# First half of the maximum scores between the transposes and the main scores, fewer VectorE instructions a step, and one pipeline stage less, in a gated cross-attention and expert layer

## What is computed

```python
x = x + tanh(g_xattn[0]) * xattn(values=ctx, keys=ctx, query=layernorm(x), w_out, b_out)
#   energy = einsum('nqhd,nkhd->nhqk', q, k);  softmax(energy / sqrt(128)) over k;  out @ w_out.T + b_out
x = x + tanh(g_ffn[0]) * ffn(layernorm(x), Wg, W1, b1, W2, b2)
#   logits = xt @ Wg; idx1, idx2 = the two best experts of a row, weighted by their gates
#   pos1 = rows before this one whose first choice is the same expert   (a running count)
#   pos2 = the same for second choices, behind all the first ones;  rows past C = 2048 are dropped
#   h = gelu(xe @ W1 + b1); ye = h @ W2 + b2; out = w1 * ye[idx1, pos1] + w2 * ye[idx2, pos2]
```

## Time and profile before

| what | value |
|---|---|
| time, median of 3 runs | 402.06 us (400.1 to 402.23) |
| time of the profiled execution | 403.13 us |
| its span in the trace | 401.3 us |
| busy in the span: TensorE matmul, VectorE, ScalarE, GpSimd | 79%, 68%, 56%, 55% |

### The profile page before, as it was taken

The page is one execution under the profiler, slowest core; times in us unless marked ns, Lnnn a source line. Parts: engine busy times, 40 slices in busy tenths (PEclk is TensorE's granted clock), DMA queues, the critical chain, the costliest instruction groups (busy, mean ns, idle before and its releaser), DMA issues.

```text
span 401.3 us, 13831 instructions
## 1 busy us (share of the span) xinstructions
PE 315.7 (79%) x4010; PEld 255.9 (64%) x4011; DVE 274.2 (68%) x1088; ACT 223.6 (56%) x660; POOL 222.2 (55%) x368
## 2 busy tenths in 40 slices
PE   0488999999999999977405999999999989998200
PEld 0246666666666666655304899999999989997100
DVE  4758999999999999975762455554555545554287
ACT  1358887777777778853011555555555555554140
POOL 4322457777777777667730455555455545454262
PEclk9999999999999999999555999999999999999855
DMA  6943432212222200100132121222122222120296
GB/s 161 296 145 108 125 119 74 78 61 73 84 80 82 82 30 30 35 30 31 45 86 47 48 59 55 64 60 65 57 62 63 62 60 56 56 59 27 84 356 189
DMA packets 40332, 33.91 MB, mean 85 GB/s; under 512 B 5046, under 2 KB 33112, under 8 KB 40288
## 3 DMA queue, kind: packets, MB, share of 16 engines
q1 hardware_dynamic: 35360, 24.65, 21.3%
q0 software_dynamic: 4352, 8.43, 6.0%
q10 hardware_dynamic: 576, 0.26, 0.3%
HBM read 18.02 MB, written 15.83 MB: 84 GB/s over the span
## 4 chain that ended last, share of the span: by engine, by line
PE 35%; POOL 19%; DMA 13%; issue 13%; DVE 8%; ACT 2%; SPq 1%; POOLq 0%; DVEq 0%; ACTq 0%
PE main_scores L667 12%; PE main_scores L681 11%; POOL expert_rows L426 11%; DMA choice_rows<-y_s,dest 9%; PE main_scores L600 3%; POOL rstd L453 3%; PE mixed L641 2%; DVE x_all L878 2%; DVE x_all L882 2%; DMA yc<-choice_rows 1%; POOL rstd L446 1%; POOL values L442 1%; POOL x_all L433 1%; PE max_scores L658 1%; PE mixed L615 1%
## 5 line engine op out<-in xcount | busy, mean ns | idle before, releaser
L466 POOL DMA_INDIRECT choice_rows<-y_s,dest x72 | 80.0, 1112 | 90.6 <-DVE y_s L859 79.0
L531 ACT ACTIVATE hT<-main_scores,ex_cur 128x128 f32<-128x128 f32 x288 | 82.3, 369 | 79.5 <-PE main_scores L667 70.9
L667 PE MATMUL main_scores<-xtT,ex_cur 128*128 128x128 f32 x576 | 81.7, 286 | 4.2 <-DVE xtT L854 3.1
L737 DVE TENSOR_REDUCE negmax<-max_scores 128x8 bf16<-128x1024 f32 x64 | 77.6, 1213 | 8.0 <-PE max_scores L568 7.9
L681 PE MATMUL main_scores<-w_sb,hT 128*128 x576 | 81.1, 284 | 0.4 <-ACT hT L531 0.4
L667 PEld LDWEIGHTS main_scores<-xtT,ex_cur 128*128 128x128 f32 x576 | 71.4, 195 | 10.2 <-DVE xtT L854 8.7
L426 POOL DMA_INDIRECT expert_rows<-xrow,slot_i x64 | 64.2, 1003 | 16.8 <-issue 16.1
L681 PEld LDWEIGHTS main_scores<-w_sb,hT 128*128 128x128 f32 x576 | 70.6, 193 | 1.8 <-issue 0.6
L849 DVE COPY ex_cur<-ex_sb 128x644 f32 x72 | 35.8, 498 | 51.2 <-issue 33.5
L513 ACT ACTIVATE probs<-main_scores 128x1024 f32<-128x1024 f32 x64 | 62.0, 1021 | 8.4 <-issue 5.0
L600 PE MATMUL main_scores<-qT,kT 32*128 32x512 f32 x256 | 38.4, 667 | 4.3 <-ACT mT L489 3.9
(11 more groups left out here) (132 smaller groups left out, 488.8 us busy)
## 6 DMA issues: line engine op xcount, KB each, us to landing
xt<-expert_rows SPq DMA_DIRECT2D x72, 64.5 KB, 1.8
choice_rows<-zeros SPq DMA_DIRECT2D x16, 256.0 KB, 2.2
yc<-choice_rows SPq DMA_DIRECT2D x16, 256.0 KB, 5.8
ex_sb<-in_L_ffn_W_dram SPq DMA_DIRECT2D x4, 512.0 KB, 5.1
w_sb<-in_L_ffn_W_dram SPq DMA_DIRECT2D x4, 512.0 KB, 4.4
out_dram<-x_all SPq DMA_DIRECT2D x8, 256.0 KB, 3.0
x_all<-in_x_dram SPq DMA_DIRECT2D x5, 384.0 KB, 6.4
ctx_all<-in_ctx_dram SPq DMA_DIRECT2D x5, 384.0 KB, 6.6
```

The source lines that it names most:

```text
L466: nc.gpsimd.indirect_dma_start(y_dram, bass.IndirectOffsetOnAxis(ap=dest[:, v, :], axis=0), y_s[:, v, :], None, bounds_check=last_row, oob ...
L531: last = nc.scalar.activation(hT[:, v % 2, c, :], H_BANK[v % 2][:, c * P:c * P + P], ACT.Gelu, bias=ex_cur[:, v, FF + D + c:FF + D + c + 1])
L667: last = nc.tensor.matmul(H_BANK[v % 2][:, c * P:c * P + P], ex_cur[:, v, c * P:c * P + P], xtT[:, v % 2, :], start=True, stop=True)
L737: V.tensor_reduce(negmax[:, m % 3, 2 * h:2 * h + 2, 0:J], S_ALL[:, :].rearrange("p (g j k) -> p g j k", g=2, j=J), AX.X, ALU.max, negate=T ...
```

## The change

It does six things in the first part, and nothing in the second.

1. `max_scores(m, 0)` is issued by TensorE between the transposes of a and the main scores of b. Before, it stood at the end of the step before, as `max_scores(a, 0)`, behind the multiplication with the values.
2. `maximum(0)` of VectorE stands behind the write of `xrow`, ahead of the layernorm's aggregation for n. Before, it stood at the head of the step.
3. The stages from b on come one step earlier (`B_AT` -2 instead of -3, ..., `D_AT` -9 instead of -10), so that the pipeline has 43 steps, not 44. `kT` and `qT` have three buffers, not four.
4. The copy of the logits to `lg` is gone. `V.max` and `V.max_index` read the bank directly, and `V.max_index` moves from the head of the next step into the same step. The transposes of the next step now wait for it (`top_idx`) where they waited for `lg_done`.
5. The two additions of the running count become one, over 32 columns instead of 16 and 16 (`places`).
6. VectorE writes the normed row once. A new copy on GpSimd, 128x128, doubles it, and the indirect DMAs wait for that copy (`row_copied`).

```diff
-        N_AT, X_AT, A_AT, M_AT, B_AT, P_AT, Q_AT, C_AT, W_AT, R_AT, K_AT, D_AT = 2, 1, 0, -1, -3, -4, -5, -6, -7, -8, -9, -10
+        N_AT, X_AT, A_AT, M_AT, B_AT, P_AT, Q_AT, C_AT, W_AT, R_AT, K_AT, D_AT = 2, 1, 0, -1, -2, -3, -4, -5, -6, -7, -8, -9
...
                     pool.wait_ge(xn2_ready, at(d, 1, 1))
+                    pool.wait_ge(row_copied, at(d, 1, 1))
...
+                if w is not None:
+                    pool.wait_ge(xn2_ready, at(w, 1, 1))
+                    nc.gpsimd.tensor_copy(xrow[:, w % NX, 1, 0:D], xrow[:, w % NX, 0, 0:D]).then_inc(row_copied, 1)
...
-                wait(pe, lg_done, gone(t, R_AT))
+                wait(pe, top_idx, gone(t, R_AT))
...
+                max_scores(m, 0)
                 if b is not None:
...
-                max_scores(a, 0)
...
-                if k is not None:
-                    wait_alone(dve, top_max, at(k, 1, 1))
-                    V.max_index(topi[:, k % 2, :], top_all[:, k, :], lg[:, k % 2, :]).then_inc(top_idx, 1)
-                maximum(0)
...
-                    V.tensor_scalar(xrow[:, w % NX, :, 0:D], x_all[:, cols(w)].unsqueeze(1).to_broadcast([P, 2, D]),
+                    V.tensor_scalar(xrow[:, w % NX, 0, 0:D], x_all[:, cols(w)],
                                     mv2[:, w % 2, 0:1], rstd2[:, w % 2:w % 2 + 1], ALU.subtract, ALU.mult).then_inc(xn2_ready, 1)
+                maximum(0)
...
-                    V.tensor_copy(lg[:, r % 2, :], LOGIT).then_inc(lg_done, 1)
+                    V.max(top_all[:, r, :], LOGIT).then_inc(top_max, 1)
...
-                    V.tensor_tensor(place[:, :, :].rearrange("p k e -> p (k e)"), PLACE, carry[:, 1 - k % 2, :], ALU.add).then_inc(place_done, 1)
-                    V.tensor_tensor(carry[:, k % 2, :], CARRY, carry[:, 1 - k % 2, :], ALU.add).then_inc(carry_done, 1)
+                    V.tensor_tensor(places[:, k % 2, :, :], M0[:, 0:4 * E].rearrange("p (u e) -> p u e", u=2),
+                                    places[:, 1 - k % 2, 1:2, :].to_broadcast([P, 2, 2 * E]), ALU.add).then_inc(carry_done, 1)
+                if r is not None:
+                    wait_alone(dve, top_max, at(r, 1, 1))
+                    V.max_index(topi[:, r % 2, :], top_all[:, r, :], LOGIT).then_inc(top_idx, 1)
...
-                if r is not None:
-                    wait_alone(dve, lg_done, at(r, 1, 1))
-                    V.max(top_all[:, r, :], lg[:, r % 2, :]).then_inc(top_max, 1)
```

21 lines of the change are left out of this document (10 added, 11 removed).

## The result

The changed kernel took 406.13 us (median of 4 runs, 404.61 to 406.95), the kernel before 401.79 us beside it (4 runs). The ratio is 1.0126, 95% interval 1.0098 to 1.0154: slower by 1.3%. The profiled execution of the changed kernel took 405.94 us, with a span of 404.1 us.

The account below looks back on a forecast made before the run. VectorE was taken to bound the kernel at 5.17 us a step. Fill +3.3, steady steps +3.6, last three +0.35 and drain -4.14 gave +3.1 us: 406.2 profiled, 405.2 median, range about 398.5 to 408.

Parts of the forecast that it names:

- Bound and wait: VectorE sets the 5.17 us step; after the change its second maximum waits 0.39 us for TensorE in every step.
- slack: Ahead of VectorE's first maximum: 1.4 us of other work against 1.2 us of TensorE work, about 0.2 us, so no wait.
- VectorE's saving: The `lg` copy, one count addition and half the `xrow` write removed: 0.22 us a step, bounds 0.15 to 0.38.
- Steady steps: The 21 steps between second maxima 7 and 28: each 0.17 us longer, +3.6 us in all.
- The TensorE loop: From the transpose of `negmax` through ScalarE and back: stays near 5.02 us, needing some 0.3 us less than the new step.
- the last three steps: The last steps with maxima, without layernorm: bounded by TensorE's 5.02 us loop, the longer first adding about +0.35 us.
- The fill: Pipeline start up to second maximum 7: rounds of 5.6 us at first, +3.3 us, put between +0.5 and +4.5.
- The rival of a cheap fill: TensorE reaches its short matmul times sooner, so the fill costs +0.5 us instead of +3.3: 402.4 us, chance 0.24.
- The drain: Emptying pipeline: one step of 4.88 us falls away, against +0.74 us for three GpSimd copies: -4.14 us.
- GpSimd's copy: The new 128x128 copy on GpSimd: taken as 0.40 us, between 0.24 and 0.47, hidden in the steady step.
- if the second part changes its length: A sign that the prediction is wrong: the second part keeps its instructions and should only move as a whole.

Follow-up runs that it names:

- l_fewer_stage: The changed kernel without edits 1 and 2, with the first part's 64 indirect DMAs moved behind the pipeline: 467.92 us, steady step 5.07 us.
- l_after: The changed kernel with the first part's 64 indirect DMAs moved behind the pipeline: 482.54 us, steady step 5.47 us.
- l_max_before_xrow: `l_after` with `maximum(0)` one instruction earlier on VectorE, ahead of `xrow`: 474.66 us, steady step 5.28 us.
- e4_max_before_xrow: The changed kernel with `maximum(0)` one instruction earlier, ahead of `xrow`, DMAs in place: 433.80 us, ratio 1.0025 to the kernel before on the same chip.
- l_before: The kernel before with the first part's 64 indirect DMAs moved behind the pipeline: 476.57 us, steady step 5.33 us.

## Why the prediction was right, and where it was wrong

**Bound and wait: right.** VectorE was the bound and is not any more. Second maximum: 0.39 us predicted, 0.40 measured from start to start (0.31 noted), in every step, and `l_fewer_stage` against `l_after` gives 0.40 for the order alone. No wait before the first maximum, as forecast, but its slack was thinner than stated: it starts 0.55 behind the first half where `l_max_before_xrow` shows that 0.45 is enough, so 0.10 and not 0.2, and one place earlier it waits.

**VectorE's saving: right, a little small.** 0.22 predicted. In step 10 of the trace after (5.31 us) the work without the wait is 4.91, so 0.26 of 5.17; the pair with the DMAs moved gives 0.26. The move of `V.max` and `V.max_index` to the accumulation bank cost nothing that a row shows. By the figures of the Trainium skill, "VectorE: DVE Perf Modes", section "The TRN2 errata — SBUF-src ops pay a fixed extra latency per instruction", it would have been an estimated 0.13 us a step; the trace after does not agree (0.17 busy, 0.08 to the next start, for both).

**Steady steps: the right number, with one part unnamed.** 5.17 - 0.26 + 0.40 = 5.31, which is what steps 8 to 11 take. From step 12 on they take 5.38: `xrow` starts 0.23 after the statistics instead of 0.21 and the maximum 0.30 after `xrow` instead of 0.24, the distance that `xrow` also has where its row notes a wait. I read this as the arrival of `rstd2`, which argues from rows; no run settled it for the steady part. Against 5.22 in the mean before, the mean after is 112.87 / 21 = 5.37: +0.16, predicted +0.17.

**The TensorE loop, and with it the last three steps: the step that failed.** The prediction said of the change that it "leaves its length alone", that this loop "stays near 5.02", and that "in the last three steps with maxima there is no layernorm to do and the TensorE loop of 5.02 bounds". They take 5.38 each. Two things were wrong. First, the loop did not stay at 5.02. The first half was fitted into the 0.36 us of waiting for `mT`, but within one and the same step the second half now has to wait for the first maximum, and that for the first half. With the new order the loop is 5.28 to 5.29 (`l_max_before_xrow`), so it needs 0.1 us less than the new step, and not 0.3. Second, `rstd2`. The last of these hand-overs, in the timeline after (the second maximum behind it is the row at 180.33 above):

```profile
177.55 0.57 POOL L456 TENSOR_TENSOR rstd<-ve,neg_half 128x1 f32<-128x1 f32 x1 [1.50 <-DVE ve L730]
...
178.23 0.39 DVE L759 TENSOR_SCALAR xrow<-x_all,mv,rstd 128x128 f32<-128x128 f32 x1 [0.39 <-POOL rstd L456]
...
178.53 1.21 DVE L740 TENSOR_REDUCE negmax<-max_scores 128x8 bf16<-128x1024 f32 x1
```

`xrow` waits 0.39 us for `rstd2`, and the second maximum 0.59 for TensorE, the whole trip of the earlier trace rows, since `mv1` and `ve1` are gone too. I had named `rstd2` as what stands behind the new copy in GpSimd's queue, and looked only at GpSimd's queue; I had not priced its cover on VectorE. From `ve2` to `xrow` VectorE had a whole first maximum to do before, 2.25 us from start to start:

```profile
129.06 0.15 DVE L727 TENSOR_SCALAR ve<-mv 128x1 f32<-128x1 f32 x1
...
131.31 0.41 DVE L760 TENSOR_SCALAR xrow<-x_all,mv,rstd 128x256 f32<-128x256 f32 x1
```

With edit 2 it has 0.92 (123.55 to 124.47), just the length of the trip (0.23 + 0.58 + 0.11). Without `xn` and its statistics it has less, and waits. The last three steps came +0.98 above the forecast (16.14 for 14.81 + 0.35). Two kernels with the DMAs moved divide that roughly in two: `l_after` takes 16.08, `l_max_before_xrow`, without `rstd2` ahead of the first maximum, 15.60, still 0.44 above the forecast's 15.16.

**The fill: right in size (+3.13 for +3.3), by rounds that came a little shorter.** The rounds were forecast at 5.6 us, second maxima at 15.5, 21.1 and 26.7; they came at 15.37, 20.63 and 25.79, and the last three steps up to maximum 7 took 5.3 to 5.45 us instead of 4.5 to 5.3, which makes up for it. The rival of a cheap fill was wrong, but each group of edits by itself makes one (-0.46 to +0.46). The term is less certain than its hit suggests: the traces of one and the same fill differ by up to 0.86. They differ where TensorE's eight matmuls fall from 0.61 us to 0.40 and, in `e4_max_before_xrow`, rise again for a while at a granted clock of 0.50 (25 to 30 us). The granted clock alone does not tell 0.61 from 0.40: it is 1.00 in every 5 us from 15 to 40 us, before and after, while the matmuls go from the one to the other in that stretch.

**The drain: -3.72 for -4.14.** The last DMA but one took 1.47 us where the others take 0.96, and that alone is more than the 0.42. GpSimd's copy takes 0.28 us and not 0.40.

**The second part: unchanged, but not to the microsecond.** It took 1.28 us less, and by its own words ("if the second part changes its length") the prediction would be wrong. Its instructions are the same, and the twelve other traces have it at 183.2 to 185.9 us, so 184.77 after is in their midst and 186.05 before is the longest of all. The difference needs no cause in the change. By the start of the load of `yc` in the chain that ended last, 0.82 of it had come together, and 0.46 came behind. So the agreement of 405.94 with the forecast of 406.2 is in part luck: it rests on two misses of opposite sign, +0.96 in the first part and -1.28 in the second.

**A better version.** Everything but edits 1 and 2 was the best of the kernels with the DMAs moved, 8.7 us faster than `l_before` (467.92 to 476.57, two chips on which the kernel before took 430.4 and 430.56). With the DMAs in place it was measured only where the long steps hide it (1.0015). Edit 3 alone was faster even there (0.9948). On a chip at 402 us neither has run. VectorE alone would allow a step of 5.17 - 0.26 = 4.91, but in the old order the TensorE loop stands at 5.02 (the last step of `l_fewer_stage` is 5.03). By 21 steps of -0.15, a fill of +0.8 and a drain of -4 it would be near 395; this is an estimate.

## What to carry to other kernels

When one instruction is moved, look at both gaps that it leaves: the one that it was filling, and the one that it now widens. Here the first maximum had covered a round trip through TensorE and, at its old place, one through GpSimd; both trips were as long as before, and each became visible. An engine that falls from 98% to 92% busy while the step grows is the sign of it: count the loop through the engines, hand-overs included, and compare it with the busiest engine's own sum. Count every loop anew when an instruction moves: here the TensorE loop grew from 5.02 to 5.28 us without one instruction more in the step, because an instruction that had been off it came to lie on it. And parts of a change do not add up in a pipeline's fill: the order that cost nothing there alone put 2.4 us on top of the earlier stage.
